# Layer one's product of adjacency and x is made in an earlier stage, kept in DRAM and loaded back

## The reference

```python
x = _layernorm(x + _L0_gnn_ref(x, adj, bias0))   # layer one
x = _layernorm(x + _L1_gnn_ref(x, adj, W_lang, W_grav, W_V, W_O, ...))
x = _layernorm(x + _L2_gnn_ref(x, adj, bias2))
x = _layernorm(x + _L3_gnn_ref(x, adj, adj, bias3))
```

```python
xw = einsum('nbl,lo->nbo', xn, weight)           # weight is adj
out = einsum('sd,sbl->dbl', An, xw) + bias
```

## Time and profile before

| | us |
|---|---|
| median of 3 runs (1785.38 to 1788.62) | 1785.61 |
| the profiled execution, its time | 1781.9 |
| its span | 1779.8 |
| TensorE busy | 1557.4 (88%) |
| DVE busy | 1286.9 (72%) |
| ACT busy | 828.6 (47%) |
| POOL busy | 548.3 (31%) |

### The profile page before, as it was taken

How to read it: one execution, slowest core, us unless ns; L and a number is a source line. 1 busy time by engine, 2 the same in 40 slices (tenths; PEclk the granted TensorE clock), 3 DMA queues, 4 the chain that set the end, 5 groups by cost and what they waited for, 6 DMA issues and landing times. The chain is left out here.

```text
span 1779.8 us, 27351 instructions
## 1 busy us (share of the span) xinstructions
PE 1557.4 (88%) x7776; PEld 1268.6 (71%) x7776; DVE 1286.9 (72%) x3046; ACT 828.6 (47%) x1381; POOL 548.3 (31%) x749
## 2 busy tenths in 40 slices
PE   7899470599999999999999999998599791799997
PEld 4678330478888888888888888876488691577775
DVE  5798799347766677666776667765477699599997
ACT  7775220134344443444434444343333591377775
POOL 5652020012123221232212322122100000599997
PEclk9999685799999999999999999999699895799998
DMA  5320200101001110011100111000442000244442
GB/s 210 106 72 1 94 0 0 47 25 42 24 30 47 47 41 23 30 47 47 41 22 31 47 47 41 18 12 25 171 143 95 0 0 0 71 144 146 145 143 106
DMA packets 57580, 106.14 MB, mean 60 GB/s; under 512 B 5888, under 2 KB 6016, under 8 KB 57536
## 3 DMA queue, kind: packets, MB, share of 16 engines
q1 hardware_dynamic: 57536, 105.60, 17.7%
HBM read 71.90 MB, written 33.69 MB: 59 GB/s over the span
## 5 line engine op out<-in xcount | busy, mean ns | idle before, releaser
L773 POOL TENSOR_TENSOR rs_a<-ve_a,neghalf 128x1 f32<-128x1 f32 x64 | 34.6, 541 | 495.4 <-DVE nm_a L767 495.4
L232 PE MATMUL acc<-xn_lo,xn_hi 128*128 128x512 f32 (+1 forms) x640 | 145.4, 358 | 5.0 <-DVE xn_lo L203 4.8
L198 ACT ACTIVATE xn_hi<-xn 128x512 fp32r<-128x512 f32 x128 | 80.6, 630 | 117.1 <-DVE xn L191 117.0
L232 PEld LDWEIGHTS acc<-xn_lo,xn_hi 128*128 128x128 f32 x640 | 102.3, 192 | 19.2 <-DVE xn_lo L203 10.4
L1566 PE MATMUL l_ps<-an_hi,xw_hi 128*128 128x512 f32 x256 | 105.5, 412 | 9.8 <-POOL xw_lo L1627 8.4
L223 PEld LDWEIGHTS acc<-xn_hi 128*128 128x128 f32 x512 | 95.6, 192 | 24.3 <-ACT xn_hi L198 7.7
L923 PE MATMUL l_ps<-an_hi,xw_hi 128*128 128x512 f32 x256 | 103.2, 403 | 6.5 <-DVE xw_lo L1263 6.3
L564 DVE MATCH_REPLACE8 work<-best,work 128x520 f32<-128x520 f32 x160 | 107.7, 685 | 0.0
L329 POOL TENSOR_TENSOR sq_lo<-sq,sq_hi 128x512 fp32r<-128x512 f32 x64 | 87.3, 1380 | 61.2 <-ACT sq_hi L296 61.0
L203 DVE TENSOR_TENSOR xn_lo<-xn,xn_hi 128x512 fp32r<-128x512 f32 x128 | 105.8, 827 | 0.4 <-ACT xn_hi L198 0.2
L923 PE MATMUL l_ps<-an_hi,xw_lo 128*128 128x512 f32 x256 | 101.3, 396 | 0.0
(11 more groups left out here) (239 smaller groups left out, 4869.5 us busy)
## 6 DMA issues: line engine op xcount, KB each, us to landing
xr<-in_x SPq DMA_DIRECT2D x32, 512.0 KB, 3.5
xin<-in_x SPq DMA_DIRECT2D x64, 256.0 KB, 2.6
between<-xo SPq DMA_DIRECT2D x64, 256.0 KB, 2.0
xres<-between SPq DMA_DIRECT2D x32, 512.0 KB, 3.7
xin<-between SPq DMA_DIRECT2D x64, 256.0 KB, 2.7
out<-xo SPq DMA_DIRECT2D x64, 256.0 KB, 2.0
raw_lang<-in_L_gnn_W_lang SPq DMA_DIRECT2D x1, 1024.0 KB, 5.5
raw_grav<-in_L_gnn_W_grav SPq DMA_DIRECT2D x1, 1024.0 KB, 7.9
```

The source lines that it names most:

```text
L198: self.nc.scalar.activation(self.hi[:, i % 4, :], self.xn[:, i % 4, :], ACT.Copy).then_inc(self.hi_ready, 1)
L232: mm = self.nc.tensor.matmul(out, h[:, c * P:(c + 1) * P], l[:, a:b], start=False, stop=False, skip_group_check=True)
```

## The change

Layer one's `xw` of all 64 batches is made in the first choosing stage. The ring `xr` now lives on through that stage; TensorE multiplies the 32 batches that lie in it ahead of the weights' work, and the other 32, loaded again from `x`, behind it. ACT copies each result from PSUM to one of four slots of `xw_sb`, and SP stores it to `xw_dram`. The middle stage loads `xw` beside x; its four `xw` products in a turn are gone, ACT and DVE read the loaded tile in place of PSUM, and the freed bank becomes a second bank for `l0`. To make room in SBUF, the tile `sq` shrinks from four slots to two, with a wait of `square` on `sq_lo`. `an_hi` and `an_lo` are allocated earlier.

```diff
@@ choose
+            xr, x, xw_dram = early
+            order = [*range(nb - RING, nb), *range(nb - RING)]
+            xw_sb = sb("xw_sb", [P, 4, N])
+            xw_ps = [ps(f"xw_ps{k}") for k in range(4)]
...
             for k in w_dram:
                 sp.dma_start(raw[k][:], w_dram[k].rearrange("(c p) n -> p c n", p=P)).then_inc(w_loaded, 16)
+            for n, b in enumerate(order):
+                sp.wait_ge(xw_out, n + 1)
+                sp.dma_start(xw_dram[b], xw_sb[:, n % 4, :]).then_inc(xw_stored[n % 4], 16)
+                if n + RING < nb:
+                    sp.dma_start(xr[:, b % RING, :], x[order[n + RING]]).then_inc(x_back[n % 4], 16)
+            for k in range(4):
+                sp.wait_ge(xw_stored[k], 16 * (nb // 4))
...
+            def early_xw(n):
+                b = order[n]
+                if n >= RING:
+                    pe.wait_ge(x_back[n % 4], 16 * ((n - RING) // 4 + 1))
+                if n >= 4:
+                    pe.wait_ge(xw_out, n - 3)
+                for c in range(CH):
+                    mm = nc.tensor.matmul(xw_ps[n % 4][:, c * P:(c + 1) * P], xr[:, b % RING, c * P:(c + 1) * P],
+                                          s.adj[:], start=True, stop=True)
+                mm.then_inc(xw_made, 1)
+            for n in range(RING):
+                early_xw(n)
             pe.wait_ge(w_loaded, 16 * len(w_dram))
...
+            for n in range(RING, nb):
+                early_xw(n)
...
+            def take_xw(n):
+                act.wait_ge(xw_made, n + 1)
+                if n >= 4:
+                    act.wait_ge(xw_stored[n % 4], 16 * (n // 4))
+                nc.scalar.activation(xw_sb[:, n % 4, :], xw_ps[n % 4][:], ACT.Copy).then_inc(xw_out, 1)
+            for n in range(RING):
+                take_xw(n)
...
@@ gnn_layer_pair
+        xw = sb("xw", [P, GRP, N])
...
-        sq = sb("sq2", [P, GRP, N])
+        sq = sb("sq2", [P, 2, N])
...
-        ht_ps = xw_ps, l0_ps = ps("xw_ps"), ps("l0_ps")
+        ht_ps = l0_ps = [ps("l0_ps0"), ps("l0_ps1")]
...
             def load(b, i):
+                sp.dma_start(xw[:, i, :], xw_dram[bass.ds(b, 1)].rearrange("a p n -> p (a n)")).then_inc(xw_in[i], 16)
...
                 def l0(i):
 
                     pe.wait_ge(xw_hi_ok, GRP * ga + i + 1)
-                    pe.wait_ge(xw_lo_ok, 1 + GRP * ga + i + 1)
-                    if not first(ga) or i:
-                        pe.wait_ge(ya_ok, GRP * ga + i)
-                    if i == 0 and not first(ga):
-                        pe.wait_ge(ht_lo_ok, GRP * ga)
+                    pe.wait_ge(xw_lo_ok, GRP * ga + i + 1)
+                    if i >= 2:
+                        pe.wait_ge(ya_ok, GRP * ga + i - 1)
+                    elif not first(ga):
+                        pe.wait_ge(ht_lo_ok, GRP * ga + i - 1)
...
                 def xw_hi_(i):
-                    act.wait_ge(xw_made, GRP * ga + i + 1)
+                    act.wait_ge(xw_in[i], 16 * (ga + 1))
                     act.wait_ge(l0_made, GRP * ga + i + 1)
-                    copy(xw_hi[:, i % 2, :], xw_ps[:]).then_inc(xw_hi_ok, 1)
+                    copy(xw_hi[:, i % 2, :], xw[:, i, :]).then_inc(xw_hi_ok, 1)
...
                 def square(i):
                     act.wait_ge(xo_ok, GRP * gp + i + 1)
-                    nc.scalar.activation(sq[:, i, :], xo[:, i, :], ACT.Square).then_inc(sq_ok, 1)
+                    act.wait_ge(sq_lo_ok, GRP * gp + i + 1)
+                    nc.scalar.activation(sq[:, i % 2, :], xo[:, i, :], ACT.Square).then_inc(sq_ok, 1)
...
+            act.sem_inc(sq_lo_ok, 2)
...
                 def xw_lo_(i):
                     dve.wait_ge(xw_hi_ok, GRP * ga + i + 1)
-                    lo_part(xw_lo[:, i % 2, :], xw_ps[:], xw_hi[:, i % 2, :], xw_lo_ok)
+                    lo_part(xw_lo[:, i % 2, :], xw[:, i, :], xw_hi[:, i % 2, :], xw_lo_ok)
```

More of the change, by code:

```diff
@@ L540, in _, with choose @@
                                                op0=ALU.mult, op1=ALU.add)
-def choose(nc, s, work, weights, xres):
+def choose(nc, s, work, weights, xres, early):
     rounds, rest = TOP // 8, TOP % 8
@@ L778, with gnn_layer_pair @@
 HILO = [(0, 0), (0, 1), (1, 0)]
[L781 removed]
+def gnn_layer_pair(nc, s, x, xw_dram, out, u_l, u_g, wov, n2):
     nb = x.shape[0]
@@ L1712, in accumulators, with adjacency @@
             return [ps(f"acc{k}") for k in range(6)]
-        def adjacency(acc, room, psum_room, weights, xres):
-            sb, _, _ = scope(nc, room)
-            s.an_hi, s.an_lo = sb("an_hi", [P, CH, N], F32R), sb("an_lo", [P, CH, N], F32R)
+        def adjacency(acc, psum_room, weights, xres, early):
             with ExitStack() as choice_room:
@@ L1722, in adjacency @@
                 psum_room.close()
-                choose(nc, s, work, weights, xres)
+                choose(nc, s, work, weights, xres, early)
                 normal_adjacency(nc, s, sim, work)
@@ L1727, in adj_resnorm_kernel @@
             acc = accumulators(psum_room)
-            first_similarity(nc, s, x, acc, consts, small)
             sb, _, _ = scope(nc, weight_room)
+            s.an_hi, s.an_lo = sb("an_hi", [P, CH, N], F32R), sb("an_lo", [P, CH, N], F32R)
             dst = {k: [sb(f"u_{k}_{p}", [P, TRI_W], F32R) for p in ("hi", "lo")] for k in ("lang", "grav")}
             dst["ov"] = [sb(f"wov_{p}", [P, CH, N], F32R) for p in ("hi", "lo")]
-            adjacency(acc, weight_room, psum_room, ({"lang": w_lang, "grav": w_grav, "v": w_v, "o": w_o}, dst), None)
-            gnn_layer_pair(nc, s, x, between, dst["lang"], dst["grav"], dst["ov"], n2)
+            with ExitStack() as x_room:
+                sb, _, _ = scope(nc, x_room)
+                xr = sb("xr", [P, RING, N])
+                first_similarity(nc, s, x, xr, acc, consts, small)
+                adjacency(acc, psum_room, ({"lang": w_lang, "grav": w_grav, "v": w_v, "o": w_o}, dst), None,
+                          (xr, x, xw_dram))
+            gnn_layer_pair(nc, s, x, xw_dram, between, dst["lang"], dst["grav"], dst["ov"], n2)
         with ExitStack() as psum_room, ExitStack() as x_room:
@@ L1738, in adj_resnorm_kernel @@
             second_similarity(nc, s, xres, acc, between, n2)
-            adjacency(acc, x_room, psum_room, None, xres)
+            s.an_hi, s.an_lo = sb("an_hi", [P, CH, N], F32R), sb("an_lo", [P, CH, N], F32R)
+            adjacency(acc, psum_room, None, xres, None)
             last_layers(nc, s, between, xres, out)
```

45 lines of the change are left out of this document (16 added, 29 removed).

## The result

The changed kernel takes 1837.63 us (median of 4 runs, 1835.19 to 1839.77), the kernel before 1785.49 (1784.99 to 1788.62) on the same chip: a ratio of 1.0292, interval 1.0272 to 1.0313. The forecast was 1820, its range 1795 to 1845. The profiled execution took 1839.35 us with a span of 1837.5, which is 57.7 above the span before.

What follows compares the result with a forecast made beforehand. It took TensorE's own work to bound the middle stage and DVE the choosing stage. Terms +18 + 18 + 8 - 9 = +35 us, against a median of 1785.6, gave a forecast of 1820 us, range 1795 to 1845.

Steps and rivals of the forecast that it cites:

- choosing stage: First choosing stage: early products, waiting on stores behind the weights, lengthen it by 18 us, all on the path; bounds 13, 27.
- the two turns ahead of the loop: Middle stage, two turns without `square`: they gain 3.5 us and 3.3 plus about 2, together -9 us; bounds -6 and -11.
- 14 turns: chain and port: Middle-stage turns: `l0(3)` comes later through waits from `sq_lo(0)` to `xw_lo(3)` and POOL's shared port; 1.3 us each, +18 us.
- 14 turns: clock: Middle-stage turns: TensorE's stop ahead of `l0(3)` sometimes drops its clock, +8 us; bounds 0 and 24.
- a third of the turns: Middle stage: the assumed portion of turns in which TensorE's clock falls, at 1.7 us each.
- rival (d): Middle stage: TensorE's clock falls in every turn, +24 us, giving 1837 us; chance 0.15.
- the upper bound: Middle stage: a clock fall in all 14 turns at 1.7 us each, 24 us.
- (a): Middle stage: removing the matmuls pays, up to 3.3 us a turn, giving 1749 us; chance 0.10.
- (b): Middle stage: the `sq_lo` wait chain costs time but port and clock do not, giving 1803 us; chance 0.17.
- (c): Choosing stage: it hides all the added work, DVE still last at 306, giving 1803 us; chance 0.08.
- the 3.3 us: Middle stage: time of the four products that leave TensorE in each turn, 4 x 0.82 us.
- the start of a turn: Middle stage: two products (1.6 us) come out there, but TensorE wins only 0.3 us; the rest becomes waiting.

Runs made afterwards that it cites:

- experiment 3: The changed kernel with twelve products of zeros ahead of `l0(3)` that keep TensorE at work while it waits: 1811.76 us.
- experiment 7: The changed kernel with SP's 32 reloads of x moved behind the first 32 stores, at most four in flight: 1824.46 us.
- Experiment 6: The changed kernel's choosing stage with the middle stage of the kernel before; the 64 early products are stored and nobody reads them: 1801.36 us.
- experiment 1: The changed kernel with `xw_hi(3)` moved ahead of `square(2)` and `square(3)` in ACT's program: 1761.51 us.
- experiment 2: The changed kernel with `sq_lo(0)` and `sq_lo(1)` moved ahead of `root_a(2)` in POOL's program: 1764.54 us.
- experiment 4: The changed kernel with POOL holding `sq_lo(2)` and `sq_lo(3)` back until DVE is through `xw_lo(3)`: 1822.64 us.
- experiment 5: The changed kernel with both the zero products ahead of `l0(3)` and POOL's `sq_lo(2)` and `sq_lo(3)` held back until `xw_lo(3)` is done: 1802.14 us.

## Why the prediction was right, and where it was not

The direction and the mechanism held. The measured 1837.6 lies in the stated range of 1795 to 1845, but above the forecast's own 1810 to 1830: the growth is 52 us where 35 were forecast. The sizes, against the span's +57.7:

| step | forecast | measured |
|---|---|---|
| choosing stage | +18 | +17.1 (`an` at 336.6, before 319.5) |
| the two turns ahead of the loop | -9 | -6.2 |
| 14 turns: chain and port | +18 (1.3 each) | +20.2 (1.44 each, experiment 3) |
| 14 turns: clock | +8 | +24.6 (1.76 each) |
| what is left, at the end | | +2.0 |

**The choosing stage** went as worked out, through each of its waits: the fifth take at 220.43 (218.7 forecast), and the weights' work through at 292.7 (292.7). Two errors cancel in that second number. The start was 1.7 us late, but the pace faster than forecast (1.29 in place of 1.5; 512 KB in 1.29 us are 406 GB/s, above the 370 that the prediction scaled up), so the 32nd take came at 256.2 and not at 259.2; then the weights' work took 3.2 us more than counted (the sum written there, 259.9 + 2.2 + 32 - 1.5, is 292.6). Half of that is the clock. The prediction let TensorE's clock stay up into this work; in the trace TensorE stops for 3.62 us behind ACT's last takes, and the products of `raw_lang` run at a granted clock of 0.84 and take 10.48 us, where they take 8.90 in experiment 7, whose stop is 0.30. The rest of the 3.2 stays open. TensorE's timeline of the changed kernel, then of experiment 7:

```profile
257.34 1.15 PE L673 MATMUL prep<-ident,raw_o 128*128 128x128 f32 x8 [3.62 <-ACT wo_t L701]
258.68 10.48 PE L680 MATMUL prep<-raw_lang 128*128 128x512 f32 x32 [0.19 <-ACT wo_t L701]
...
248.21 1.15 PE L684 MATMUL prep<-ident,raw_o 128*128 128x128 f32 x8 [0.30 <-ACT wo_t L712]
249.55 8.90 PE L691 MATMUL prep<-raw_lang 128*128 128x512 f32 x32 [0.20 <-ACT wo_t L712]
```

The last 32 batches took no more than forecast, with two short waits for their own stores. Experiment 6 shows the cost by itself: 16.8.

**The turn** went as written, instruction by instruction: `square(2)` behind `sq_lo(0)`, `xw_hi(3)` behind both squares, `xw_lo(3)` blocked by POOL, `l0(3)` last. TensorE's stop was forecast at 3.3 us and is 3.25. Experiments 1 and 2 break the chain at either end, and each gives all of it back and more. Of the 1.44 us, the port is 0.69 (forecast 0.75) and the chain 0.75 (forecast 0.55). `xw_lo` takes 1.34 us beside POOL, 0.68 to 0.69 without; the rule of the Trainium skill that the prediction weighed, page "SBUF — State Buffer", section "Who interferes with whom", holds in this trace.

**The clock** is the term that was mis-sized: forecast +8, measured +24.6. The prediction named both bounds and the price of one fall (1.7 us, measured 1.76), and then took a third of the turns. It fell in all of them: rival (d), which gave 1837 and had a chance of 0.15. That the rival's time is met within 1 us is in part luck: its terms add up to +51, and the profiled executions differ by 57.7.

The reason for the third was one row, a stop of 2.76 us in another stage that "left the clock up". The row doesn't show that. TensorE's timeline of the kernel before around this stop has matmuls of the same form before and behind it:

```profile
18.18 0.77 PE L216 MATMUL scale<-rows,sel 128*128 128x512 f32 x1
...
24.10 0.74 PE L216 MATMUL scale<-rows,sel 128*128 128x512 f32 x1
...
27.76 0.44 PE L216 MATMUL scale<-rows,sel 128*128 128x512 f32 x1
```

`scale` takes 0.77 us ahead of the stop and 0.77 and 0.74 behind it, as it does at 50.10 (0.79) behind the stop of 3.80, where the granted clock is 0.51 from 50 to 52 us; from 27.76 on it takes 0.44. So these matmuls were as slow as at the lower level before the stop began, and the row says nothing of what a stop does to a clock that is up. The profile's windows do give a granted clock of 1.00 for this stretch; in the trace of experiment 4, where the first three `scale` take 0.77, 0.76 and 0.73 us, they give 0.50. A granted clock this early in a trace has to be checked against the lengths of matmuls. In the loop, where the clock was up beforehand, stops of 3.21 to 3.25 us were followed by a fall 14 times of 14, and stops of 2.53 to 2.59 (experiment 4) 13 times of 14.

So the upper bound was the better reading. The Trainium skill, page "TensorE: Matmul & The Clock Gate", section "HAM oscillation — how this bites in real kernels", describes a kernel in which a wait for DMA in each pass of a loop drops the clock in each pass. This trace agrees, for waits on other engines: 14 falls in 14 turns. The turns of a loop are nearly alike; here the clock fell in all turns, in all but one, or, where the stop was gone (experiments 1 and 3), in none. A third of them was a mean over two cases, not a likely case.

**The two turns ahead of the loop** gained 2.6 and 3.6, by the turned product of the first (373.06, before 358.56) and `xw_hi(0)` of the loop (426.23, before 415.32), where 3.5 and 5.3 had been counted. TensorE waits there for DVE's and ACT's chain with or without the products, as in the loop.

**The rivals.** (a), that the matmuls pay, was wrong for this kernel and right for its neighbour: with the wait moved aside the loop is 2.1 us a turn faster than before. (b) is experiment 5, at 1802. (c), that the choosing stage hides it all, is refuted by experiment 6. The share of the 3.3 us that is had there is 2.1. Most of the other 1.2 is what the prediction said of the start of a turn. In experiment 1 TensorE stands there twice, which it doesn't in the kernel before:

```profile
694.74 0.47 PE L969 MATMUL y_l<-ht_hi,u_lang_hi 128*128 128x512 f32 x1 [0.53 <-issue]
...
699.73 0.66 PE L1027 MATMUL tr<-ident,k_g 128*128 128x128 f32 x4 [0.31 <-DVE k_g L1402]
```

These are `yprod(0)` and `k_turned`, together 0.84 us; an edit that takes them away was not tried, and the last 0.4 was not traced. Giving `sq` its four slots back, which would remove the wait itself, was not tried either.

## What to carry to other kernels

When an edit shrinks a buffer, the new wait costs little where it stands and much through what is queued behind it: list the instructions behind it on the same engine, and move the one that another engine waits for ahead of it before judging the edit. In a loop, cost a possible fall of the clock as all turns or none; forecast one of the two and keep the other as a rival. A row that shows a clock staying up is evidence only if matmuls ahead of the stop were fast. A 1 MB load placed between the stores of a ring of four slots cost 4 to 5 us each time; in one block ahead of the stores four of them cost one wait of 9 to 10 us, and on another engine's queue one of 4.4. Count waits, not bytes.

## What the hardware showed that was not expected

- TensorE's clock fell to the lower level behind each of 14 stops of 3.21 to 3.25 us and cost 1.76 us a turn; in the turn shown it was low until the ninth matmul (3.7 us). It fell behind 13 of 14 stops of 2.53 to 2.59 us too, at once in one turn, six matmuls later in another, and once not at all.
- The windows of two traces gave a granted clock of 1.00 and of 0.50 for the same early stretch (9 to 26 us) though its matmuls took the same time to 0.01 us in both (`scale`: 0.77, 0.77 and 0.74 against 0.77, 0.76 and 0.73).
- Twelve products of zeros (2.90 us) in the gap brought 25.9 us.
- One queue moved a store and a load of 256 KB each in 1.29 us, 406 GB/s, in most of the changed kernel's first 32 takes.
- A store of 256 KB behind 4 MB of loads on its queue held its successor for 10.30 us; with the loads on another engine's queue, 4.38 us.
